# A shifted-window attention kernel: one maximum for two steps, scores a step ahead, attention output on two column tiles of 64, and x's high part read in place

## The reference, cut to what matters

```python
# stage 1: Swin window attention, windows of 7 x 7, shift 3, 12 heads of 8
qkv  = xw @ qkv_w.T + qkv_b                  # xw: (32*64 windows, 49, 96)
attn = q * 8**-0.5 @ k.T + bias + mask       # 49 x 49 for each head
out  = softmax(attn) @ v @ proj_w.T + proj_b
# stage 2: divisive normalisation with box sums of width 5 and 20
s   = box(x, width 5); num = box(s * s, channels 20)
d   = box(box(x * x, width 5), channels 20)
out = num / (d * count)
```

## Time and profile before

| what | us |
|---|---|
| median of 3 runs | 3128.87 |
| lowest, highest | 3127.85, 3129.82 |
| the profiled execution's own time | 3126.64 |
| its span | 3124.8 |
| PE busy | 2972.2 |
| DVE busy | 2838.5 |
| POOL busy | 2657.3 |
| ACT busy | 2252.2 |

### The profile page before, as it was taken

The page is one execution under the profiler, slowest core; times in us unless marked ns, Lnnn a source line. Parts: engine busy times, 40 slices in busy tenths (PEclk is TensorE's granted clock), DMA queues, the critical chain, the costliest instruction groups (busy, mean ns, idle before and its releaser), DMA issues.

```text
span 3124.8 us, 196803 instructions
## 1 busy us (share of the span) xinstructions
PE 2972.2 (95%) x85120; PEld 2397.8 (77%) x85120; DVE 2838.5 (91%) x4883; ACT 2252.2 (72%) x4705; POOL 2657.3 (85%) x2974
## 2 busy tenths in 40 slices
PE   4999999999999999999999999999999999999995
PEld 2777787777787777777777777777787777787773
DVE  5999999999999999999999999999999999999993
ACT  2577777777777777777777777777777777777764
POOL 4588889888889888889888889888889888889886
PEclk8999999999999999999999999999999999999995
DMA  3333343333333333333343343333343334333330
GB/s 83 90 93 91 95 98 91 93 97 91 95 98 92 96 95 90 94 98 90 92 99 90 92 99 90 92 98 92 93 98 91 91 91 99 94 94 86 80 73 25
DMA packets 385895, 283.39 MB, mean 91 GB/s; under 512 B 261931, under 2 KB 384908, under 8 KB 385036
## 3 DMA queue, kind: packets, MB, share of 16 engines
q1 hardware_dynamic: 384652, 270.69, 35.4%
q10 hardware_dynamic: 384, 0.11, 0.0%
HBM read 39.35 MB, written 38.54 MB: 25 GB/s over the span
## 4 chain that ended last, share of the span: by engine, by line
PE 83%; ACT 7%; issue 5%; POOL 3%; DVE 1%; SPq 1%; DMA 0%; ACTq 0%; POOLq 0%; DVEq 0%
PE pP L480 21%; PE pO L496 15%; PE pS L468 11%; PE pM L450 6%; PE pM L519 5%; PE pM L574 4%; PE pM L408 3%; PE pM L409 3%; PE pM L410 3%; PE pM L402 3%; PE pM L509 2%; PE pM L597 2%; PE pM L567 1%; PE pM L568 1%; ACT X L649 1%
## 5 line engine op out<-in xcount | busy, mean ns | idle before, releaser
L1081 POOL TENSOR_TENSOR T<-T,MX 128x588 f32<-128x588 f32 x1024 | 1207.6, 1186 | 414.0 <-DVE MX L843 413.0
L678 ACT ACTIVATE P<-pP 128x588 f32<-128x588 f32 x1024 | 673.9, 658 | 530.4 <-PE pP L480 523.9
L480 PE MATMUL pP<-K,T 113*128 113x113 f32 x6144 | 821.4, 270 | 4.6 <-POOL T L1081 1.8
L836 DVE TENSOR_TENSOR T<-pS,table 128x588 f32<-128x588 f32 x1024 | 779.6, 761 | 36.7 <-PE pS L468 35.3
L843 DVE TENSOR_REDUCE MX<-T 128x12 f32<-128x588 f32 x1024 | 778.4, 760 | 26.0
L480 PEld LDWEIGHTS pP<-K,T 113*128 113x128 f32 x6144 | 603.4, 141 | 99.1 <-issue 4.6
L496 PEld LDWEIGHTS pO<-V,P 128*32 128x32 f32 (+1 forms) x49152 | 507.3, 103 | 180.7 <-issue 73.6
L496 PE MATMUL pO<-V,P 128*17 128x18 f32 (+1 forms) x49152 | 612.9, 184 | 18.0 <-issue 17.0
L468 PE MATMUL pS<-KE,QS 128*64 128x196 bf16 (+1 forms) x8192 | 478.8, 234 | 21.4 <-DMA KE<-KS 14.8
L468 PEld LDWEIGHTS pS<-KE,QS 128*64 128x64 bf16 x8192 | 293.3, 108 | 55.3 <-DMA KE<-KS 15.3
L668 ACT ACTIVATE V<-pM 49x384 f32<-49x384 f32 x512 | 265.2, 518 | 54.2 <-PE pM L450 47.0
(11 more groups left out here) (105 smaller groups left out, 6264.5 us busy)
## 6 DMA issues: line engine op xcount, KB each, us to landing
KE<-KS SPq DMA_DIRECT2D x512, 147.0 KB
KS<-knh SPq DMA_DIRECT2D x768, 49.0 KB
QS<-qnh SPq DMA_DIRECT2D x768, 49.0 KB
out<-tok_out SPq DMA_DIRECT2D x384, 84.0 KB
tok_in<-x SPq DMA_DIRECT2D x224, 84.0 KB
KS<-knl SPq DMA_DIRECT2D x384, 49.0 KB
QS<-qnl SPq DMA_DIRECT2D x384, 49.0 KB
tok_in<-x SPq DMA_DIRECT2D x224, 63.0 KB
```

What stands on the lines that cost most here:

```text
L480: mm = pe.transpose(pP[:, c, QN * at:QN * at + QN], T[j % 4][0:QN, 2 * h:2 * h + 2, :], pick)
L678: act.activation(P32[j % 3][:, :, :].rearrange("p (c a w) q -> p c a (w q)", c=2, w=2), src, ACT.Exp).then_inc(p_made, 1)
L836: dve.tensor_tensor(T[j % 4][:, :, 0:L].rearrange("p (b h) k -> p b h k", b=2), pS[:, :, 0:HALF].rearrange("p b (h k) -> p b h k", k=L), t ...
L1081: pool.tensor_tensor(t, t, MX[j % 4][:, :].unsqueeze(2).broadcast_to([128, HEADS, L]), ALU.subtract).then_inc(shifted, 1)
```

## The change

There are four edits.

1. **One maximum for two steps.** `T` and `MX` become three double buffers (`T2`, `MX2`), whose halves are the six buffers of steps. `maxima(pair)` takes both steps in one DVE instruction, in the slot of the second. That slot is odd (1 or 3).
2. **Scores a step ahead.** `scores(j)` and `add_bias(j)` are in slot `j - 2` and no longer in `j - 1`. `shift(j)` stays in slot `j - 1`, `turn_scores(j)` in `j + 1`.
3. **Attention output on two column tiles of 64.** The two matmuls for queries 0 to 31 and 32 to 48 become one for all 49.
4. **x's high part read in place.** `XH` is now a view of the upper halves of the float32 words of X (every second bf16), X has a 97th row of ones, and POOL's copy `high_x` is gone. `low_x` subtracts the cut value and not the rounded one. The set-up fills both X tiles with ones, in place of XH, and the last row of XL with zeros.

```diff
@@ -43,7 +43,7 @@
 
 
 
-LOAD_AT, FILL_AT, STATS_AT, HIGH_AT, LOW_AT = -78, -50, -49, -29, -23
+LOAD_AT, FILL_AT, STATS_AT, LOW_AT = -78, -50, -49, -23
 QK_AT, V_AT, O_AT, TURN_O_AT, PROJ_AT, X1_AT, X1_STATS_AT = -15, 0, 6, 7, 8, 9, 11
 STAGE_AT = -13
 
@@ -158,8 +158,8 @@
         table = [sb(f"table{i}", [128, SC]) for i in range(4)]
 
         tok_in = [sb(f"tok_in{i}", [2 * SIDE, 4, C]) for i in range(LOADS)]
-        X = [sb(f"X{i}", [C, UNITS * TOK]) for i in range(2)]
-        XH = sb("XH", [C + 1, UNITS * TOK + 16], BF16)
+        X = [sb(f"X{i}", [C + 1, UNITS * TOK]) for i in range(2)]
+        XH = [t[:, :].bitcast(BF16).rearrange("c (t half) -> c t half", half=2)[:, :, 1] for t in X]
         XL = sb("XL", [C + 1, UNITS * TOK + 16], BF16)
 
         qn = [[sb(f"qn{p}{i}", [C, 2 * TOK], BF16) for i in range(2)] for p in "hl"]
@@ -170,8 +170,9 @@
         KS = sb("KS", [128, HG, 2 * TOK], BF16)
         KE = [sb(f"KE{i}", [128, HEADS, 2 * TOK], BF16) for i in range(2)]
         V = [sb(f"V{i}", [128, UNITS, HP, 2, D + 1]) for i in range(2)]
-        T = [sb(f"T{i}", [128, HEADS, 64]) for i in range(4)]
-        MX = [sb(f"MX{i}", [128, HEADS]) for i in range(4)]
+        T2 = [sb(f"T{i}", [128, 2, HEADS, 64]) for i in range(3)]
+        MX2 = [sb(f"MX{i}", [128, 2, HEADS]) for i in range(3)]
+        T, MX = ([pair[i // 2][:, i % 2] for i in range(6)] for pair in (T2, MX2))
         P32 = [sb(f"P32{i}", [128, HEADS, L]) for i in range(3)]
         bias_raw = P32[0][:, :, :].rearrange("p h k -> p (h k)").rearrange("p (k h) -> p k h", h=HEADS)
         rden = sb("rden", [128, PAIRS * HEADS])
@@ -402,12 +402,12 @@
                     mm = pe.transpose(bankA[0:C, at:at + 2 * SIDE], tok_in[U % LOADS][:, t, :], roll[0:2 * SIDE, :])
                 mm.then_inc(xT_made, 1)
 
-            def project(dst, col, u, done):
+            def project(dst, col, m, u, done):
 
                 xs = slice(TOK * u, TOK * u + TOK)
-                pe.matmul(dst[0:C, 0:TOK], WH[:, col:col + C], XH[:, xs], start=True, stop=False)
+                pe.matmul(dst[0:C, 0:TOK], WH[:, col:col + C], XH[m % 2][:, xs], start=True, stop=False)
                 pe.matmul(dst[0:C, 0:TOK], WH[:, col:col + C], XL[:, xs], start=False, stop=False)
-                pe.matmul(dst[0:C, 0:TOK], WL[:, col:col + C], XH[:, xs], start=False, stop=True
+                pe.matmul(dst[0:C, 0:TOK], WL[:, col:col + C], XH[m % 2][:, xs], start=False, stop=True
                           ).then_inc(done, 1)
 
             def qk(U):
@@ -442,7 +442,7 @@
                 for w in range(2):
                     for p in range(PAIRS):
                         at = TOK * u + L * (2 * p + w)
-                        xh, xl = XH[:, at:at + L], XL[:, at:at + L]
+                        xh, xl = XH[m % 2][:, at:at + L], XL[:, at:at + L]
                         col = (2 * p + w) * C // 2
                         for part, (lhs, rhs) in enumerate(((xh, WHV), (xh, WLV), (xl, WHV))):
                             for h in range(2):
@@ -477,7 +477,7 @@
                     pe.wait_ge(p_made, j)
                 for h in range(HP):
                     c, at = divmod(h, HP // 2)
-                    mm = pe.transpose(pP[:, c, QN * at:QN * at + QN], T[j % 4][0:QN, 2 * h:2 * h + 2, :], pick)
+                    mm = pe.transpose(pP[:, c, QN * at:QN * at + QN], T[j % 6][0:QN, 2 * h:2 * h + 2, :], pick)
                 mm.then_inc(turned, 1)
 
             def times_v(j):
@@ -492,9 +492,8 @@
                 for h in range(HP):
                     col = VC * (HP * p + h)
                     for w in range(2):
-                        for q0, q1 in ((0, 32), (32, L)):
-                            mm = pe.matmul(pO[64 * w + q0:64 * w + q1, col:col + VC], P32[j % 3][:, 2 * h + w, q0:q1],
-                                           V[U % 2][:, 2 * p + w, h, :, :], start=True, stop=True)
+                        mm = pe.matmul(pO[64 * w:64 * w + L, col:col + VC], P32[j % 3][:, 2 * h + w, :],
+                                       V[U % 2][:, 2 * p + w, h, :, :], start=True, stop=True)
                 mm.then_inc(pv_made, 1)
 
             def turn_o(U):
@@ -603,7 +602,7 @@
             for s in range(FIRST_SLOT, END_SLOT + 1):
                 for j in steps(s - 3):
                     times_v(j)
-                for j in steps(s + 1):
+                for j in steps(s + 2):
                     scores(j)
                 for U in units(s, V_AT):
                     values(U)
@@ -829,18 +828,19 @@
             def add_bias(j):
                 U, p = divmod(j, PAIRS)
                 dve.wait_ge(scores_made, j + 1)
-                if j >= 4:
-
-                    dve.wait_ge(turned, j - 3)
+                if j >= 6:
+
+                    dve.wait_ge(turned, j - 5)
                 tab = table[2 * (U % UNITS == UNITS - 1) + (p == PAIRS - 1)]
-                dve.tensor_tensor(T[j % 4][:, :, 0:L].rearrange("p (b h) k -> p b h k", b=2),
+                dve.tensor_tensor(T[j % 6][:, :, 0:L].rearrange("p (b h) k -> p b h k", b=2),
                                   pS[:, :, 0:HALF].rearrange("p b (h k) -> p b h k", k=L),
                                   tab[:, :].rearrange("p (b h k) -> p b h k", b=2, k=L), ALU.add
                                   ).then_inc(biased, 1)
 
-            def maximum(j):
-                dve.wait_ge(biased, j + 1)
-                dve.tensor_reduce(MX[j % 4][:, :], T[j % 4][:, :, 0:L],
+            def maxima(pair):
+                dve.wait_ge(biased, 2 * pair + 2)
+                dve.tensor_reduce(MX2[pair % 3][:, :, :].rearrange("p t h -> p (t h)"),
+                                  T2[pair % 3][:, :, :, 0:L].rearrange("p t h k -> p (t h) k"),
                                   AX.X, ALU.max).then_inc(maxed, 1)
 
             def low_q(U):
@@ -988,15 +988,16 @@
                     result(G)
                 for U in units(s, O_AT):
                     divide_o(U)
-                for j in steps(s + 1):
+                for j in steps(s + 2):
                     add_bias(j)
                 for U in units(s, STATS_AT):
                     stats_of_x(U)
                 for U in units(s, X1_AT):
                     if U % UNITS == UNITS - 1:
                         stats_of_x1(U)
-                for j in steps(s + 1):
-                    maximum(j)
+                for j in steps(s + 2):
+                    if j % 2:
+                        maxima(j // 2)
                 for U in units(s, X1_STATS_AT):
                     if U % UNITS < UNITS - 1:
                         stats_of_x1(U)
@@ -1012,20 +1013,14 @@
 
         @block.gpsimd
         def _(pool):
-            def high_x(U):
+            def low_x(U):
                 m, u = divmod(U, UNITS)
                 s = slice(TOK * u, TOK * u + TOK)
                 pool.wait_ge(x_kept, U + 1)
                 if m:
 
                     pool.wait_ge(v_made, U - UNITS + 1)
-                pool.tensor_copy(XH[0:C, s], X[m % 2][:, s]).then_inc(xh_made, 1)
-
-            def low_x(U):
-                m, u = divmod(U, UNITS)
-                s = slice(TOK * u, TOK * u + TOK)
-                pool.wait_ge(xh_made, U + 1)
-                pool.tensor_tensor(XL[0:C, s], X[m % 2][:, s], XH[0:C, s], ALU.subtract).then_inc(xl_made, 1)
+                pool.tensor_tensor(XL[0:C, s], X[m % 2][0:C, s], XH[m % 2][0:C, s], ALU.subtract).then_inc(xl_made, 1)
 
             def pairs_of_y(G):
                 pool.wait_ge(y_made, G + 1)
@@ -1076,20 +1071,20 @@
                                      ).then_inc(wrapped, 1)
 
             def shift(j):
-                pool.wait_ge(maxed, j + 1)
-                t = T[j % 4][:, :, 0:L]
-                pool.tensor_tensor(t, t, MX[j % 4][:, :].unsqueeze(2).broadcast_to([128, HEADS, L]),
+                pool.wait_ge(maxed, j // 2 + 1)
+                t = T[j % 6][:, :, 0:L]
+                pool.tensor_tensor(t, t, MX[j % 6].unsqueeze(2).broadcast_to([128, HEADS, L]),
                                    ALU.subtract).then_inc(shifted, 1)
 
-            zero = [*tok_in, P32[0], XL, V[0], V[1], T[0], T[1], T[2], T[3], O[0], O[1], Y,
+            zero = [*tok_in, P32[0], XL, V[0], V[1], *T2, O[0], O[1], Y,
                     SQ, ybox2, SQ_low, ybox2_low]
-            one = [XH, OT]
+            one = [*X, OT]
             for t in zero:
                 pool.memset(t[tuple([slice(None)] * len(t.shape))], 0.0).then_inc(pool_fills, 1)
             for t in one:
                 pool.memset(t[tuple([slice(None)] * len(t.shape))], 1.0).then_inc(pool_fills, 1)
             pool.wait_ge(pool_fills, len(zero) + len(one))
-            pool.memset(XH[0:C, UNITS * TOK:], 0.0).then_inc(ones_ended, 1)
+            pool.memset(XL[C:C + 1, :], 0.0).then_inc(ones_ended, 1)
 
             for s in range(FIRST_SLOT, END_SLOT + 1):
                 for G in groups(s, BOX_AT):
@@ -1108,8 +1103,6 @@
                         wrap(U)
```

(13 more changed lines are left out.)

## The result

The changed kernel takes 3204.5 us (median of 4 runs, 3197.2 to 3207.3) where the kernel before takes 3129.4 (4 runs, 3127.9 to 3132.7): the ratio is 1.0223, 95% interval 1.0202 to 1.0244. By the medians it is 75 us slower (by the ratio 70); 102 were forecast. First its page: the engines' shares and the chain, as in the earlier trace rows.

A forecast was written before the change was run, and what follows sets the result against it. PE, busy 95%, was taken as the bound. Terms 23 (edit 3) + 72 (edit 1) + 2 (edit 2) + 0 (edit 4) + 5 (set-up) = 102 us on 3126.64, plus 2.2 to the median, gave 3231 us; range 3155 to 3270.

The forecast's parts named there:

- mechanism, place: Slot 3: the double maximum on DVE stands ahead of L929, so PE's L519 waits; 72 us.
- 4.0 said: L929's counterpart was to start 4.0 us after the end of slot 3's scores, 3.7 before.
- 0.32: Slot 3: L929 comes 0.60 - 0.28 = 0.32 us later against PE's scores, and L519 waits for all of it.
- 224: Number of units with a group (32 x 7) in which PE pays the delay of L929; 72 us in all.
- The rival that it is paid nowhere: DVE catches up, L929 keeps its place and the double maximum costs nothing: 3159 us; chance 0.13 (maximum hidden).
- Edit 3's interval: Attention output: successive float32 loads and matmuls of 49 columns on one tile come 46 ns apart (41 + 5).
- 768 x 0.03 = 23: Attention output: PE's list grows 0.03 us a step, paid in 768 steps outside the V slot: 23 us.
- The rivals of 27 and of 38 ns a load: Attention output's loads come faster: 27 ns, wide tiles win, 3070 us, chance 0.10; 38 ns, 3163 us, chance 0.10.
- 1.8 us of slack remain: Every eighth step, scores read KE a step earlier, still 1.8 us after its loads land; cost taken as 2 us.
- the nearest row: Matmuls reading x in place: strided weights load in 99 ns like packed ones, so the strided read costs 0.
- Half rate: Rival: matmuls read the strided moving operand at half rate, 167 us more, 3398 us; chance 0.05.
- The set-up was 5 by the fills: Set-up: two fills of X replace XH's, plus a row of XL, 2 x 2.7 = 5 us more on the path.

The follow-up runs named there:

- the shifted pairs: Changed kernel with the double maximum moved to slots 0 and 2, behind the ratio's operations: 3156.5 us, ratio 1.0102 to the kernel before.
- edit 3 alone: Kernel before with only the attention output put on two column tiles of 64: 3112.4 us against 3123.8, ratio 0.9960.

## Why the prediction was right, and where its terms were not

The time was 27 us under the forecast and inside the range. The terms, in us:

| term | forecast | found |
|---|---|---|
| edit 3 | +23 | -12: +34 for the tiles, -46 from issue |
| edit 1 | +72 | +50 by the ratios, 56 by the starts |
| edit 2 | +2 | +21 |
| edit 4 with the set-up | +5 | +11 |
| sum | +102 | +70 by the ratios, 75 by the medians |

- **Edit 1 was right in mechanism, place and nearly in size.** L929 came 4.01 us behind the scores (4.0 said). PE pays 0.25 ahead of L518 and 0.04 in it, not 0.32, and in 204 units, not 224. The rival that it is paid nowhere falls with the shifted pairs.
- **Edit 3's interval was exact, the sign of its term was wrong.** 46 ns a load, on a measured pair; the first interval cost 20 ns more, 0.044 a step, not 0.03. The step that failed is "768 x 0.03 = 23": it left out what half as many instructions give back. The rows stood in view: "issue" 5% of the chain, and issue behind the V matmuls in the earlier trace rows. The rivals of 27 and of 38 ns a load fall.
- **Edit 2** was the term most in error for its size: "1.8 us of slack remain" is right for the steady state, but in the first and last units KE came 1.1 to 3.0 us late four times, and each time half clock stood behind the wait. Neither the lateness at either end nor the clock was in the sum.
- **Edit 4:** the nearest row, a strided weight load, was taken for a strided moving operand; that costs 7 ns in 330. Half rate falls. The Trainium skill (SBUF — State Buffer, Door 1: The DMA port swizzle) has reads at full rate with two or more hits in a 16-byte line, by which the cost is 0; the rows show 2% more, and they decide. The set-up was 5 by the fills and 4.3 by the first scores.
- That the sum came so near is in part luck. Its errors cancelled in part: -35 at edit 3, -16 to -22 at edit 1, +19 at edit 2, +6 at edit 4.

## What to carry to other kernels

- When the busiest engine has many short instructions, look for waits on issue and at the instruction queue's bytes: an edit that halves the instructions can pay for matmuls that are each slower.
- A longer operation costs by its place. Find the operation whose end another engine waits for, count what stands ahead of it, and put the long one behind it.
- Before work is moved to hide a wait, read which neighbour shares its tile mode. And check the ramp and the drain apart from the steady state: four waits of 1.1 to 3.0 us there, 8.5 us in all, were followed by half clock and cost 23.

## What the runs showed of the hardware

- PE stops at the borders of 16 KB blocks of its program, up to 1.3 us at a time, some 46 us in this kernel; most stops end 1.2 to 1.65 us behind the end of a packet of its instruction queue. Fewer instructions end them, fewer other transfers took a quarter off the listed waits. The 15 runs of the kernel before spread over 15 us on one chip, the 6 of edit 3 alone over 2.3.
- A float32 load and matmul on one column tile recur every 46 ns with 49 columns (tiles of 64) and every 32 ns with 32 columns (tiles of 32); the first interval of a group is 20 ns longer; going from 32-wide to 64-wide tiles takes 76 ns.
- A moving operand of bf16 at a stride of two costs 7 ns more for 392 columns.
